# Pair sums of one head in eight move from GpSimd to TensorE in a product-key FFN

## What is computed

```
x  = x + attention(layernorm(x))                 # band of 128 to each side
z  = layernorm(x)
q  = batchnorm(z) @ w_q.T                        # 8 heads x 2 halves x 128
sim = einsum(q, keys)                            # 2 halves x 8 heads x 32 keys
sx, sy = top8(sim[0]), top8(sim[1])              # per token and head
scores, pk = top8(sx[:, None] + sy[None, :])     # 8 best of 64 pairs
w_down, w_up = key_in[idx], key_out[idx]         # idx = ix * 32 + iy, of 1024 experts
o  = gelu(z . w_down) * softmax(scores)
x  = x + einsum(o, w_up)
```

## Time and profile before

| | |
|---|---|
| Time, median of 3 runs | 1811.86 us (1811.05 to 1820.54) |
| Profiled execution | 1817.61 us, span 1815.9 us, mean granted TensorE clock 0.958 |
| TensorE matmul busy | 1536.1 us, 85% of the span |
| VectorE busy | 1481.7 us, 82% |
| GpSimd busy | 1332.3 us, 73% |
| ScalarE busy | 1268.6 us, 70% |

### The profile page before, as it was taken

The page is one execution under the profiler, slowest core; times in us unless marked ns, Lnnn a source line. Parts: engine busy times, 40 slices in busy tenths (PEclk is TensorE's granted clock), DMA queues, the critical chain, the costliest instruction groups (busy, mean ns, idle before and its releaser), DMA issues.

```text
span 1815.9 us, 37722 instructions
## 1 busy us (share of the span) xinstructions
PE 1536.1 (85%) x11712; PEld 1091.8 (60%) x11712; DVE 1481.7 (82%) x3720; ACT 1268.6 (70%) x1741; POOL 1332.3 (73%) x1579
## 2 busy tenths in 40 slices
PE   3899999999999999768887888878878788887877
PEld 2455555555556666346666766666666666666656
DVE  3668888788888887159899988989889898898988
ACT  1156666666666666558888878888888888788885
POOL 1045555555555555569999999999999999999993
PEclk9689999999999999879999998999999999999999
DMA  5334444443444442100000000000000000000000
GB/s 141 76 81 98 99 97 95 101 96 95 103 103 103 99 99 56 43 29 1 19 18 1 19 18 18 0 18 18 1 18 18 11 8 18 18 0 18 13 6 7
DMA packets 73406, 85.14 MB, mean 47 GB/s; under 512 B 9856, under 2 KB 63616, under 8 KB 68608
## 3 DMA queue, kind: packets, MB, share of 16 engines
q1 hardware_dynamic: 73312, 84.08, 19.7%
HBM read 58.10 MB, written 25.95 MB: 46 GB/s over the span
## 4 chain that ended last, share of the span: by engine, by line
POOL 24%; issue 19%; DVE 7%; ACT 5%; PE 1%; POOLq 0%; DVEq 0%; ACTq 0%; SPq 0%
POOL SUM L751 24%; DVE W L944 4%; ACT E L852 3%; ACT L786 1%; DVE M8Y L888 0%; PE WT L1012 0%; DVE SMALL L888 0%; DVE SMALL L905 0%; ACT GE L785 0%; DVE CT L927 0%; ACT SIM L779 0%; ACT BNT L794 0%; PE MB L979 0%; DVE Z L911 0%; PE E L967 0%
## 5 line engine op out<-in xcount | busy, mean ns | idle before, releaser
L751 POOL TENSOR_TENSOR SUM<-SIM 128x1024 f32<-128x1024 f32 x512 | 959.9, 1912 | 39.8 <-DVE W L944 36.1
L944 DVE SCALAR_TENSOR_TENSOR W<-SUM,SMALL,E 128x1024 f32<-128x1024 f32 x512 | 646.1, 1280 | 86.2 <-ACT E L852 82.1
L852 ACT ACTIVATE E<-SUM,NB 128x1024 f32<-128x1024 f32 x512 | 567.4, 1118 | 136.1 <-DVE W L944 121.6
L1012 PE MATMUL WT<-idf,W 128*128 128x128 f32 x4096 | 554.3, 285 | 104.2 <-DVE CT L927 53.5
L1012 PEld LDWEIGHTS WT<-idf,W 128*128 128x128 f32 x4096 | 476.3, 147 | 274.8 <-DVE W L944 143.0
L264 POOL TENSOR_SCALAR_AFFINE_SELECT PT<-PT 128x128 f32<-128x128 f32 (+1 forms) x1024 | 336.4, 353 | 323.4 <-ACT PT L354 287.2
L409 DVE TENSOR_REDUCE mx<-SX 128x2 f32<-128x512 f32 x256 | 175.4, 685 | 102.7 <-PE SX L492 102.0
L411 DVE TENSOR_REDUCE mx<-SY 128x2 f32<-128x768 f32 x256 | 242.7, 948 | 7.7 <-PE SY L492 7.3
L354 ACT ACTIVATE PT<-TX 128x512 f32<-128x512 f32 x256 | 152.8, 597 | 102.2 <-PE TX L519 100.9
L356 ACT ACTIVATE PT<-TY 128x768 f32<-128x768 f32 x256 | 207.0, 808 | 2.0 <-PE TY L519 0.8
L488 PE MATMUL SY<-K,Q 72*128 72x384 bf16 x512 | 164.0, 343 | 15.6 <-DVE mx L411 14.9
(11 more groups left out here) (111 smaller groups left out, 1671.1 us busy)
## 6 DMA issues: line engine op xcount, KB each, us to landing
K<-k_parts SPq DMA_DIRECT2D x96, 192.0 KB
Q<-q_parts SPq DMA_DIRECT2D x288, 64.0 KB
q_parts<-qp SPq DMA_DIRECT2D x16, 384.0 KB, 2.4
k_parts<-kp SPq DMA_DIRECT2D x16, 384.0 KB, 2.4
xin<-in_x SPq DMA_DIRECT2D x16, 256.0 KB, 3.1
xres<-in_x SPq DMA_DIRECT2D x16, 256.0 KB, 9.0
x<-X SPq DMA_DIRECT2D x16, 256.0 KB, 2.3
x2T<-X2T SPq DMA_DIRECT2D x16, 256.0 KB, 2.1
```

The source lines that it names most:

```text
L751: return eng.tensor_tensor(SUM[(q * FH + h) % RING][:, :].rearrange("p (i j) -> p i j", i=NK), sx, sy, ALU.add)
L852: nc.scalar.activation(E[h % 2][:, :], SUM[(k * FH + h) % RING][:, :], ACT.Exp, bias=NB[q][:, h:h + 1]).then_inc(S["exp_ready"], 1)
L944: nc.vector.scalar_tensor_tensor(out=W[h % WRING][:, :], in0=SUM[(k * FH + h) % RING][:, :], scalar=TOP[q][:, h, TOPK - 1:TOPK], in1=E[h % ...
L1012: o = pe.matmul(WT[:, e, :], W[h % WRING][:, e * P:(e + 1) * P], ident[:, :], is_transpose=True, start=(h == 0 and e % 4 == 0), stop=(h == ...
```

## The change

TensorE makes the 1024 sums of head PEH = 4 of each tile, and GpSimd those of the other seven. For this the order in `KM`, and so in `SIM`, becomes head, half, key: the 64 similarities of one head then lie side by side. In head 2's slot of tile j TensorE turns 128 columns of the next tile's `SIM` (heads 4 and 5) into `MB[:, 128:256]`, ahead of the output product; ScalarE copies the first 64 partitions of that to `SIMT`, ahead of the output copy. In head 2's slot of the next tile, behind its output product and mask 2, two matmuls of `SIMT` (64 x 128) with the constant `PAIRS` (64 x 1024, ones at i and at 32 + j for column 32 i + j) put the 1024 sums of head 4 into `E[0]`, where mask 2 has freed the place. Exponential 4 reads `E[0]` in PSUM and writes `W[4]` in SBUF; mask 4 compares `E[0]` and multiplies `W[4]` in place. `SUM` has 14 buffers instead of 16. `PAIRS` is made by one GpSimd instruction from the identity matrix.

```diff
@@ attention, merging the keys
+                        at = (g % FH * 2 + g // FH) * NK
-                        o = pe.matmul(mb[:, g * NK:(g + 1) * NK], WQF[:, g, :], KT[...], start=True, stop=True)
+                        o = pe.matmul(mb[:, at:at + NK], WQF[:, g, :], KT[...], start=True, stop=True)
@@ constants and buffers
-RING = 16
+PEH = 4
+POOLED = FH - 1
+RING = 2 * POOLED
-    SIM = [sb(f"SIM{b}", [P, 2, FH, NK]) for b in range(4)]
+    SIM = [sb(f"SIM{b}", [P, FH, 2, NK]) for b in range(4)]
+    SIMT = [sb(f"SIMT{b}", [2 * NK, P]) for b in range(2)]
+    PAIRS = sb("PAIRS", [2 * NK, NE])
@@ GpSimd
+        xs = ident[0:2 * NK, 0:NK].unsqueeze(2).broadcast_to([2 * NK, NK, NK])
+        ys = ident[0:2 * NK, NK:2 * NK].unsqueeze(1).broadcast_to([2 * NK, NK, NK])
+        nc.gpsimd.tensor_tensor(PAIRS..., xs, ys, ALU.add).then_inc(S["pairs_set"], 1)
                 for h in range(FH):
+                    if h == PEH:
+                        continue
@@ ScalarE
+        def simT_copy(j, k):
+            act.wait_ge(S["sim_turned"], j + 1)
+            wait_pos(act, S["pe_sums"], j - 1)
+            nc.scalar.copy(SIMT[k % 2][:, :], MB[0:2 * NK, P:2 * P]).then_inc(S["simT_copied"], 1)
...
         sim_copy(2, 2)
+        simT_copy(0, 0)
...
+                    if h == COPY_OUT and nxt:
+                        simT_copy(j + 1, k + 1)
                     if h == COPY_OUT and (real or k):
                         finish(...)
...
+                    if h == PEH:
+                        act.wait_ge(S["pe_sums"], j + 1)
+                        wait_pos(act, S["weights_turned"], j * FH + h - WRING + 1)
+                        nc.scalar.activation(W[h % WRING][:, :], E[h % 2][:, :], ACT.Exp, bias=NB[q][:, h:h + 1])...
+                    else:
+                        act.wait_ge(S["pair_sums"], j * POOLED + pooled(h) + 1)
@@ VectorE
+                    sums, exps = (E[h % 2], W[h % WRING]) if h == PEH else (sum_of(k, h), E[h % 2])
+                    nc.vector.scalar_tensor_tensor(out=W[h % WRING], in0=sums, scalar=..., in1=exps, op0=ALU.is_ge, op1=ALU.mult)...
@@ TensorE
+        def turn_sims(j, k):
+            pe.matmul(MB[:, P:2 * P], SIM[k % 4][:, PEH:PEH + 2, :, :]..., ident[:, :], is_transpose=True, ...)
+        def pe_sums(j, k):
+            for u in range(2):
+                o = pe.matmul(E[PEH % 2][:, u * GN:(u + 1) * GN], SIMT[k % 2][:, :], PAIRS[:, u * GN:(u + 1) * GN], ...)
...
+                    if h == SLOT_OUT:
                         pe.wait_ge(S["sim_copied"], ...)
                         pe.wait_ge(S["expert_copied"], ...)
                         wait_pos(pe, S["out_copied"], j - 1)
+                        pe.wait_ge(S["simT_copied"], j + 1)
+                    if h == SLOT_OUT and (more or k < GT - 1):
+                        turn_sims(j + 1, k + 1)
+                    if h == SLOT_OUT and real:
                         outputs(...)
                     if h == SLOT_SIM and (more or k < 1):
...
+                        pe.wait_ge(S["simT_copied"], j + 2)
                         similar(...)
...
                     pe.wait_ge(S["weights_masked"], j * FH + h + 1)
+                    if h == PEH - 2:
+                        pe.wait_ge(S["simT_copied"], j + 1)
+                        pe_sums(j, k)
```

## The result

The changed kernel is slower: 1881.76 us, median of 4 runs (1870.02 to 1884.38). The ratio to the kernel before is 1.035, 95% interval 1.0327 to 1.0372. The forecast was 1852 us, ratio 1.022, with a range up to 1876. The direction was right; the size was not, and the time lies outside the range. The ratio is taken over fast runs alone (a fourth run of the kernel before, 1967.81 us, was slow); the two medians printed, 1881.76 and 1811.86, would give 1.039.

The account below looks back on a forecast made before the run. VectorE was taken to set odd tiles, ScalarE's gelu even ones, GpSimd neither. Terms 39.4, -1.5, +0.75, -4, +1.3, +3 and +1 gave +40 us on the median 1811.86: 1852 us, 2.2% slower, range 1820 to 1876.

Parts of the forecast that it names:

- The stall in odd tiles: 31 odd tiles: mask 4 starts 1.13 us later behind exponential 4, mask 5 0.14 more; 1.27 us each, 39.4 us.
- the forecast's path: Odd tile: output product, turn, sums to 950.38, exponential 4 to 951.46, mask 4 at 951.57 and not at 950.44.
- The slope of an exponential over 512 and 768 elements: Exponential 4, PSUM to SBUF: 597 ns for 512 and 808 for 768 elements, so 1.02 us for 1024.
- nearly full but not over: TensorE in odd tiles: busy time goes from 12.4 to about 14.4 us, which the longer tile still holds.
- the rival "hidden": Odd tiles: stall vanishes if sums take 1.02 us and output product clears 0.3 us sooner; 1812 us, chance 0.07.
- -1.5 foreseen: 15 even tiles k = 2 with a gelu: sums hidden, the shorter exponential gives back 0.1 us each.
- +0.75 and -4 foreseen: 15 even tiles k = 0: added copy costs 0.05 us each; CT's waits for turns shrink by two thirds, -4 us.
- The last group's tile without gelu: One of two even tiles without gelu, taken at half an odd tile's 1.27 us; +1.3 us for both.
- The prologue: Ahead of the first small exponential: an added turn and copy with hand-overs, under 1.5 us, taken as +1.
- GpSimd paced it: Rival for the whole FFN: tiles fall from 16.0 us to VectorE's 14.2, so 1697 us, faster; chance 0.06.
- Low clock in odd tiles: Rival on TensorE: sums at the lower clock cost 1.6 us more an odd tile, 1868 to 1902 us; chance 0.14.
- Cheap sums of 64 rows: Rival on TensorE's sums: one record a matmul, 1.02 us, so about 1825 us, slower by less; chance 0.11.

Follow-up runs that it names:

- the run with seven sums: The kernel before, but GpSimd makes seven sums a tile and head 4 reads head 3's sums again, nothing else added: 1812.55 us, ratio 0.9995.
- the written-out kernel: The changed kernel with the FFN's loop over pairs of groups written out, same instructions otherwise: 1856.05 us, ratio 1.0236 to the kernel before.
- the padded kernel before: The kernel before with 20 or 48 always satisfied waits a tile written into TensorE's program: 1813.88 us, ratio 1.0008, and 1810.49 us, ratio 0.9983.

## Why the prediction was right and wrong

**What bounds.** Right: GpSimd was not the bound; the run with seven sums shows it. Odd tiles set by VectorE and even ones by ScalarE's gelu: right, the even ones didn't move.

**Where the sums stand: the mechanism right, the term too small.** The stall in odd tiles was put at 1.27 us a tile and measures 1.59 to 1.6 (15.92 less 14.32; 16.0 less 14.4 with k = 3). All that is missing lies ahead of mask 4, which starts 8.94 us behind CT's start and not 8.60 as the forecast's path has it. The sums start 0.08 us later than reckoned. They were taken as 1.88 us and take 1.98, since the records start 0.43 us apart but the second starts 0.53 behind the first (0.10). Exponential 4 starts 0.11 us behind them and not 0.06 (0.05). It was taken as 1.02 us and takes 1.117 (0.10). Between mask 4 and the next CT 0.13 us more were lost, where 0.14 were foreseen. Over the odd tiles outside back jumps and the last group, 0.33 us or a little less in each, that is some 9 us.

The slope of an exponential over 512 and 768 elements was a poor guide to 1024 elements. The rule of the Trainium skill that I weighed ("ScalarE: Activation LUTs", section "Step-by-step: what each stage is for": PSUM is the faster place to write) doesn't show in this pair, 1118 ns from SBUF into PSUM and 1117 ns from PSUM into SBUF. The pair turns the place read and the place written at once, so no run here tests the rule alone, though its direction would have given the better forecast.

**TensorE "nearly full but not over": too kind.** I added busy times and found room in a tile of 15.6 us. Turns, output, similarity and expert products hang on CT, on masks and on ScalarE's copies, so room by the sum isn't room in the order. With the sums in the same place but half as long the odd tile is 15.06 us; with all of them ahead of the output product and read by nobody it is 15.06 too, by a wait of mask 5; with them ahead and read it is 15.70, by a wait of CT for turns. Each place makes its own wait. How much of the 1.6 us TensorE's load would cost without any wait of ScalarE for it, no run shows. Cheap sums and an output product out of the way, the two conditions of the rival "hidden", weren't met: the sums take 1.98 us, and moving them ahead took the wait of mask 4 to 0.23 us and brought the one of CT.

**Left out: the back jumps.** No term of the sum and no rival had them: they were put at nothing without a reason. Five k = 3 tiles are 2.1 us over their like (1.8 before, so +1.5 in all), and four k = 0 tiles 3.2 to 4.4 us over theirs, 14.7 us. Written out, the kernel loses both. This is the largest single miss. Without the 14.7 us the time would have been about 1867; without the 9 us of the stall, about 1873; either is inside the range, so it took both to leave it. What TensorE waits for in the late tiles is not in its operations. In the kernels without these pauses whose loop is kept, q8 brings TensorE no packet while the loop runs round (none from 1050 to 1690 us in the kernel before and with half the sums). In the changed kernel nine come in each iteration from the second of these jumps on, and the first two fall in the pause. So TensorE's loop body is fetched anew behind these jumps, and the pause comes with the first of it; that TensorE stands still for just these packets is argued from the times. The packets as such cost nothing: the written-out kernel has 67 and no such pause. What makes a loop body be fetched again stays open; its size alone is contradicted by the padded kernel before. Which engine's jump makes the 1.8 us of a k = 3 tile, no run separates.

**Even tiles.** k = 2: -1.5 foreseen, -1.25 measured, without the last group's. k = 0: +0.75 and -4 foreseen, -2.8 measured, with the late ones counted as 17.33 us; the granted clock of such a tile is 1.00 now, where it was 0.90, and CT waits 1.4 us for turns where it was 6.2. The last group's tile without gelu lost 2.25 us, not 0.65, and the two odd tiles of the last group 2.7 and 2.9, where 1.3 and 3 were foreseen: about 3 us short. The prologue cost nothing that shows: the first CT starts at 816.82 us, 0.42 us sooner than before. But what lies ahead of it varies: in the other runs the first CT starts anywhere from 809 to 822 us.

**The sum again.** The forecast's 40 us, 9 for the stall, 1.5 and 14.7 for the back jumps and 3 for the last group make 68; small terms, the prologue above all, take back the 1 us or so to the measured 66.8.

**The rivals.** GpSimd paced it: no, 0.9995 with seven sums. Low clock in odd tiles: no, 1.00. Cheap sums of 64 rows: no, four records in 1.98 us.

## What to carry to other kernels

An engine that is hardly ever idle, and then only because its buffers are full, is a producer and not the bound; before work is taken from it, look who waits for it. Work moved to an engine with idle time needs room at its place in the order, between the event that lets it start and the one that waits for it, and that room must be counted for the whole chain of the cycle, not by busy shares. And when instructions are added inside a loop, look at its back jumps, and try it written out.

## What the runs showed of the hardware

- A float32 matmul of 512 columns over 64 rows leaves two records 0.43 us apart, as one over 128 rows does; four of them took 1.98 us.
- An exponential of 128 x 1024 takes 1118 ns from SBUF into PSUM and 1117 ns from PSUM into SBUF.
- A back jump of the FFN's loop cost the tile that holds it 1.8 us in the kernel before (16.2 for 14.4), 2.1 in the changed one. Written out, the kernel before ran at 0.993 of its time.
- Behind back jumps TensorE paused up to 4.7 us in some programs and not in others that differ by a few instructions a tile. The first have 73 to 84 packets of its instructions on q8, nine in an iteration with a pause; the others have 36 to 38, and none from 1050 to 1670 us.
